# Two attention layers on one core: the attention output and its sums turned by 32x32 block transposes

## The reference

```python
# layer 0: 8 heads of 64, linear attention
q = softmax(q over d);  k = softmax(k over n)
att = einsum('bnhd,bnhl->bhdl', k, v);  y = einsum('bnhd,bhdl->bnhl', q, att)
x = x + silu(ln(y) * (1 + scale) + shift) @ W_out + b_out

# layer 1: 16 heads of 32, full attention over the 512 tokens of a batch
att = softmax(einsum('bnhl,bmhl->bnmh', q, k) + (1 - mask) * -1e6, axis=m)
y = einsum('bnmh,bmhl->bnhl', att, v)
out = x + silu(ln(y) * (1 + scale) + shift) @ out_w + out_b
```

## Time and profile before

| | us |
|---|---|
| median of 3 executions | 1419.43 |
| lowest and highest | 1418.87, 1429.26 |
| the profiled execution's own time | 1421.4 |
| its span, from first to last instruction | 1419.6 |

### The profile page before, as it was taken

One profiled execution on the slowest core, in us unless ns is written; L12 is line 12 of the kernel. 1 busy time (PEld: TensorE's weight loads), 2 busy tenths in 40 slices (PEclk: granted clock), 3 DMA queues, 4 the chain that ended last, 5 costly groups with the idle time before them and its releaser, 6 DMA issues.

```text
span 1419.6 us, 20550 instructions
## 1 busy us (share of the span) xinstructions
PE 1345.7 (95%) x7040; PEld 971.0 (68%) x7040; DVE 1005.0 (71%) x1966; ACT 821.8 (58%) x1429; POOL 770.8 (54%) x692
## 2 busy tenths in 40 slices
PE   6899999999999899999999999999999999999887
PEld 4678888888888786566666665666666666666445
DVE  5788978778788876677657657657757756756645
ACT  4255455454554644756756756756756766666663
POOL 0323243332433515467657757757847847846863
PEclk9899999999999999999999999999999999999999
DMA  9021111311213275745545535534634634633602
GB/s 336 1 67 53 46 60 38 97 60 38 68 37 111 91 216 172 221 135 161 143 132 160 156 119 163 165 119 145 182 120 139 182 104 142 200 105 112 180 14 82
DMA packets 82888, 172.93 MB, mean 122 GB/s; under 512 B 7240, under 2 KB 7240, under 8 KB 82784
## 3 DMA queue, kind: packets, MB, share of 16 engines
q1 hardware_dynamic: 82784, 171.62, 39.3%
HBM read 104.45 MB, written 67.14 MB: 121 GB/s over the span
## 4 chain that ended last, share of the span: by engine, by line
PE 65%; DVE 14%; DMA 7%; ACT 6%; issue 3%; POOL 3%; SPq 1%; DVEq 0%; POOLq 0%; ACTq 0%
PE ps L508 13%; PE ps L510 12%; PE ps L509 12%; PE ps L665 6%; PE ps L720 6%; PE ps L682 6%; DVE cT L1213 5%; PE ps L503 4%; DMA Ks<-stack_scratch 4%; PE ps L698 2%; DVE st L1052 2%; POOL yb L1392 2%; PE ps L596 1%; PE ps L617 1%; ACT xTh L786 1%
## 5 line engine op out<-in xcount | busy, mean ns | idle before, releaser
L1376 POOL TENSOR_TENSOR Pb<-Pb 128x512 f32<-128x512 f32 x376 | 470.2, 1289 | 218.4 <-PE ps L720 218.2
L1213 DVE TENSOR_REDUCE cT<-ps 128x1 f32<-128x512 f32 x512 | 326.2, 685 | 131.1 <-PE ps L665 126.3
L930 ACT ACTIVATE Pb<-ps 128x512 f32<-128x512 f32 x512 | 285.9, 602 | 190.3 <-PE ps L682 184.2
L665 PE MATMUL ps<-Ks,Qs 98*128 98x512 f32 x512 | 194.9, 419 | 10.9 <-DMA Ks<-stack_scratch 8.3
L682 PE MATMUL ps<-Qs,Ks 106*128 106x512 f32 x512 | 199.2, 415 | 2.3 <-ACT Qs L913 1.4
L665 PEld LDWEIGHTS ps<-Ks,Qs 98*128 98x128 f32 x512 | 95.4, 191 | 70.9 <-DVE cT L1213 21.4
L682 PEld LDWEIGHTS ps<-Qs,Ks 106*128 106x128 f32 x512 | 95.2, 190 | 50.7 <-issue 25.4
L1299 POOL TENSOR_TENSOR rs<-ve,mhalf 128x4 f32<-128x4 f32 x32 | 33.0, 1032 | 167.8 <-DVE ve L1038 115.3
L1327 POOL TENSOR_TENSOR vt<-vt,qmx 128x512 f32<-128x512 f32 x32 | 33.7, 1055 | 166.1 <-DVE qmx L1130 166.1
L508 PE MATMUL ps<-xTh,Wh_k 128*128 128x512 f32 x256 | 106.5, 416 | 3.6 <-DVE xTl L1065 2.3
L508 PE MATMUL ps<-Wh_o,sTh 128*128 128x512 f32 x256 | 106.3, 415 | 0.2 <-DVE sTl L1191 0.2
(11 more groups left out here) (176 smaller groups left out, 2956.1 us busy)
## 6 DMA issues: line engine op xcount, KB each, us to landing
Qs<-stack_scratch SPq DMA_DIRECT2D x32, 768.0 KB
Ks<-stack_scratch SPq DMA_DIRECT2D x32, 768.0 KB
stack_scratch<-sg_q SPq DMA_DIRECT2D x32, 512.0 KB, 2.7
stack_scratch<-sg_k SPq DMA_DIRECT2D x32, 512.0 KB, 2.8
wr<-in_x SPq DMA_DIRECT2D x32, 256.0 KB, 4.8
x_scratch<-wr SPq DMA_DIRECT2D x32, 256.0 KB, 2.0
stack_scratch<-sg_q SPq DMA_DIRECT2D x32, 256.0 KB, 2.9
stack_scratch<-sg_k SPq DMA_DIRECT2D x32, 256.0 KB, 3.5
```

The costliest lines, as they stand in the source:

```text
L665: e.matmul(bank[:], Qs[par][0:RX, j, t * 128:(t + 1) * 128], Ks[par][0:RX, j, :], start=True, stop=True).then_inc(s["S"], 1)
L930: e.activation(p_buf(n, m)[:, j, :], ps[bank_of["a", n, m, j]][:], ACT.Exp).then_inc(s["P"], 1)
L1213: e.tensor_reduce(nx[:, n % 2, j, t, 0:1], ps[bank_of["S", n, j, t]][:], AX.X, ALU.max, negate=True).then_inc(s["S_max"], 1)
L1376: e.tensor_tensor(acc[:, j, :], acc[:, j, :], p_buf(n, m)[:, j, :], ALU.add).then_inc(s["Ps_pool"], 1)
```

## The change

**Column tiles.** In `pv` each head's v is now loaded into all four column tiles, and column tile u takes the 128 tokens 128u to 128u+127 of that head: 16 matmuls with 128 moving columns for each m in place of 4 with 512. `den` does the same, with a `sel` that puts head h into row h of each quadrant. The bank `PV` then holds, in the 32 partitions of quadrant u, the 32 channels of head j at columns 128j and on, for the tokens of run u.

**Block transposes.** One DVE instruction turns the 32x32 blocks of `PV` straight into `yb` (`tl`, now DVE alone), and one turns the first 128 columns of `DEN` into `dt` in SBUF (`tlx`), from which the reciprocals are taken. The ACT copies L938, L946, L951 and the TensorE transposes behind them go.

**Order of the tokens.** After the block transposes, partition p = 32u + r of tile t holds token 128u + 32t + r. So that `x`, `k` and `v` stand in that order too, layer 1 loads its input from a second scratch `x1p`, which layer 0 stores beside `x1d`; the masks of layer 1 are turned on the host. The residual and the output keep the tokens' own order.

**Plan.** All of `PLAN`'s rows for layer 1 are new, and some for layer 0.

```diff
-    "tl": (0.2, 0.1, 0.9), "tlx": (1.0, 0.0, 0.4, 0.4, 0.4, 0.4),
+    "tl": (0.3,), "tlx": (0.1, 0.3, 0.4, 0.4, 0.4, 0.4),
...
-    "tl": (None, (0, 0.931), (0, 0.654), (0, 0.723)),
+    "tl": (None, (0.073, 1.091), (0.239, 0.802), (0.102, 0.771)),
...
+        x1p = nc.dram_tensor("x1_order_scratch", [B, 4, NT, 32, D], F32, kind="Internal").ap()
...
-        yt = vt[1]
+        dt = vt[1][:, 0:128]
...
                 for j in range(4):
-                    r = e.matmul(DEN[32 * j:32 * j + 32, :], sel[:, 4 - g:36 - g], p_buf(n, 0)[:, j, :],
-                                 start=(g == 0), stop=(g == NG - 1))
+                    h = 4 * g + j
+                    for u in range(4):
+                        r = e.matmul(DEN[32 * u:32 * u + 32, 0:128], sel[:, H1 - 1 - h:H1 + 31 - h],
+                                     p_buf(n, 0)[:, j, 128 * u:128 * u + 128], start=(h == 0), stop=(h == H1 - 1))
...
-                        r = e.matmul(PV[32 * j:32 * j + 32, :], xbuf(8 + b)[:, m, h * 32:(h + 1) * 32], pb[:, j, :],
-                                     start=(m == 0), stop=(m == NT - 1))
+                        for u in range(4):
+                            r = e.matmul(PV[32 * u:32 * u + 32, 128 * j:128 * j + 128], xbuf(8 + b)[:, m, h * 32:(h + 1) * 32],
+                                         pb[:, j, 128 * u:128 * u + 128], start=(m == 0 and j == 0),
+                                         stop=(m == NT - 1 and j == 3))
...
-            def tl(i, n):
-                b, g = divmod(n, NG)
-                if i == 1:
-                    e.wait_ge(s["yT"], n + 1)
-                    turn(PV, [yt[:, t * 128:(t + 1) * 128] for t in range(NT)]).then_inc(s["y1_tr"], 1)
...
-            def ae(i, n):
...
-                e.wait_ge(s["PV"], 4 * n + 4)
-                e.copy(yt[:], PV[:]).then_inc(s["yT"], 1)
...
+            def tl(i, n):
+
+                b, g = divmod(n, NG)
+                e.wait_ge(s["s_lo"], 4 * (7 + b) + g + 1)
+                e.wait_ge(s["PV"], 4 * n + 4)
+                e.transpose(yb[:, :, g * 128:(g + 1) * 128].rearrange("p t (j d) -> p j t d", j=4),
+                            PV[:].rearrange("p (j t r) -> p j t r", j=4, t=NT)).then_inc(s["y1"], 1)
+
             def tlx(i, b):
+                if i == 0:
+                    if b:
+                        e.wait_ge(s["rd"], b)
+                    e.wait_ge(s["den"], 4 * b + 4)
+                    e.transpose(dt, DEN[:, 0:128]).then_inc(s["dT"], 1)
...
-                    e.reciprocal(rd.rearrange("p t g j -> p t j g"),
-                                 DEN[:].rearrange("p (t j l) -> p t j l", t=NT, j=4)[:, :, :, 0:4]).then_inc(s["rd"], 1)
+                    e.reciprocal(rd, dt.rearrange("p (t h) -> p t h", t=NT)[:, :, 0:H1]).then_inc(s["rd"], 1)
...
-                src = (A["x"] if x < 8 else x1d)[x % 8]
+                src = A["x"][x] if x < 8 else x1p[x - 8].rearrange("u t r d -> (u t r) d")
...
+            def stored(x):
+
+                return 32 * min(x, B) + 16 * max(x - B, 0)
...
                     e.dma_start(dst[x % 8, t * 128:(t + 1) * 128, :], wr[t][:]).then_inc(s[f"st{t}"], 16)
+                    if x < 8:
+                        e.dma_start(x1p[x, :, t, :, :], wr[t][:]).then_inc(s[f"st{t}"], 16)
```

More of the change, by code:

```diff
@@ L368, in cond_two_layers @@
             "S", "S_max", "nx_set", "nx_hi", "nx_neg", "nx_lo", "nx_tr", "nxq", "ST", "P", "PV", "Ps_pool", "Ps_dve",
-            "yT", "y1_tr", "y1", "den", "dT", "d1_tr", "rd", "y1_sc")}
+            "y1", "den", "dT", "rd", "y1_sc")}
         def xbuf(x):
@@ L719, in pv @@
                         h = 4 * g + j
-                        r = e.matmul(PV[32 * j:32 * j + 32, :], xbuf(8 + b)[:, m, h * 32:(h + 1) * 32], pb[:, j, :],
-                                     start=(m == 0), stop=(m == NT - 1))
+                        for u in range(4):
+                            r = e.matmul(PV[32 * u:32 * u + 32, 128 * j:128 * j + 128], xbuf(8 + b)[:, m, h * 32:(h + 1) * 32],
+                                         pb[:, j, 128 * u:128 * u + 128], start=(m == 0 and j == 0),
+                                         stop=(m == NT - 1 and j == 3))
                     r.then_inc(s["PV"], 1)
-            def tl(i, n):
-                b, g = divmod(n, NG)
-                if i == 1:
-                    e.wait_ge(s["yT"], n + 1)
-                    turn(PV, [yt[:, t * 128:(t + 1) * 128] for t in range(NT)]).then_inc(s["y1_tr"], 1)
-            def tlx(i, b):
-                if i == 1:
-                    e.wait_ge(s["dT"], b + 1)
-                    turn(DEN, [yt[:, t * 128:(t + 1) * 128] for t in range(NT)]).then_inc(s["d1_tr"], 1)
             parts = {"m": m, "mb": mb, "tx": tx, "k": k, "v": v, "te": te, "q": q, "st": state, "y": y, "ty": ty, "o": o,
-                     "qk": qk, "S": S, "nxt": nxt, "a": a, "pv": pv, "den": den, "tl": tl, "tlx": tlx}
+                     "qk": qk, "S": S, "nxt": nxt, "a": a, "pv": pv, "den": den}
             for p, i in order:
@@ L930, in a @@
                 e.activation(p_buf(n, m)[:, j, :], ps[bank_of["a", n, m, j]][:], ACT.Exp).then_inc(s["P"], 1)
-            def ae(i, n):
-                if n:
-                    e.wait_ge(s["y1_tr"], n)
-                if n and n % NG == 0:
-                    e.wait_ge(s["d1_tr"], n // NG)
-                e.wait_ge(s["PV"], 4 * n + 4)
-                e.copy(yt[:], PV[:]).then_inc(s["yT"], 1)
-            def tl(i, n):
-                if i == 2:
-                    b, g = divmod(n, NG)
-                    if g == 0:
-                        e.wait_ge(s["s_lo"], 4 * (8 + b))
-                    e.wait_ge(s["y1_tr"], n + 1)
-                    e.copy(yb[:, :, g * 128:(g + 1) * 128], t4(PV)).then_inc(s["y1"], 1)
-            def tlx(i, b):
-                if i == 0:
-                    e.wait_ge(s["den"], 4 * b + 4)
-                    e.copy(yt[:], DEN[:]).then_inc(s["dT"], 1)
             parts = {"w": w, "nx": nx_, "ny": ny, "tx": tx, "k": k, "te": te, "v": v, "q": q, "sta": sta, "y": y, "ty": ty,
-                     "early": early, "stacks": stacks, "qk": qk, "nxt": nxt, "a": a, "ae": ae, "tl": tl, "tlx": tlx}
+                     "early": early, "stacks": stacks, "qk": qk, "nxt": nxt, "a": a}
             for p, i in order:
@@ L1565, in end @@
                 for t in range(4):
-                    e.wait_ge(s[f"st{t}"], 16 * 16)
+                    e.wait_ge(s[f"st{t}"], stored(16))
             prologue()
@@ L1585, in col, with turned @@
         return v.reshape(-1, 128).T
+    def turned(m):
+        return np.ascontiguousarray(m.reshape(B, NT, 4, 32).transpose(0, 2, 1, 3).reshape(B, T))
     def mcol(m):
@@ L1593 @@
         "m0": g["mask_BxSx1_fk1"].reshape(B, T),
-        "m1": g["mask_BxS_ff1"],
+        "m1": turned(g["mask_BxS_ff1"]),
         "mk": mcol(g["mask_BxSx1_fk1"]),
-        "mk1": mcol(g["mask_BxS_ff1"]),
+        "mk1": mcol(turned(g["mask_BxS_ff1"])),
         "cT": np.ascontiguousarray(g["cond_2048"].T.reshape(8, 128, B).transpose(1, 0, 2)),
```

48 lines of the change are left out of this document (24 added, 24 removed), and 14 rows, old and new, of the table PLAN.

## The result

The changed kernel takes 1460.62 us (median of 4 runs, 1453.65 to 1463.60). The kernel before, run beside it, takes 1422.68. The ratio is 1.0255, with an interval of 1.0197 to 1.0313: it is slower, by some 38 us, where the prediction's sum had 18 us of gain, and it lies outside the range given.

The account below looks back on a forecast made before the run. TensorE was taken as the limit, busy 95% of the span. Terms -20.0 - 4.1 + 4 + 2 + 1 - 1.1 = -18.2 from 1421.4 gave 1403.2, or 1401 us against the runs' median; range 1384 to 1424 us.

Parts of the forecast that it names:

- The second stores: Layer 0's 32 extra DMAs of 256 KB: +1 us, 3 without cover at the change of layers.
- What goes: TensorE loses 40 sets of transposes of PV and DEN, 20.0 us, and 4.1 us idle ahead of them.
- the gain is taken back by the queues: Rival: TensorE's waits move under the new plan and half the 24.1 us returns; no change, 1412 us; chance 0.20.
- What is added on TensorE: pv and den in four times as many matmuls, same columns: 3 ns for each of 1280 rounds, +4 us.
- the slow case: In pv and den, rounds too short to hide loads or issue; begun if 32 pv rows take over 1.02 us.
- short passes too short: Rival in pv and den: 0.11 us rounds cannot hide loads or issue; 1538 us with whole load exposed; chance 0.13.
- What is added on VectorE: Block transposes, 32 large at 0.69 us and 8 small at 0.30, delaying maxima TensorE waits for: +2 us.
- The new waits: On VectorE, the transpose waits for PV and GpSimd's s_lo, with the next group's maxima behind it; part of the VectorE step.
- the waits go as well: Rival: waits for turned sums and reciprocals shorten and half of TensorE's for maxima go; 1388 us; chance 0.12.
- The last stretch: Between the end of the sums and the reciprocal, a 0.30 us block transpose replaces 1.40 us: -1.1 us.
- The forecast of a batch, 106.6 us: Sign: a batch of layer 1 takes some 106.6 us in place of 109.
- layer 0 at 490 us: Sign of the prediction being right: layer 0 at 490 us.

Follow-up runs that it names:

- e2: The kernel before with only the second stores added, as the changed kernel issues them; nothing reads them: 1476.98 us, ratio 1.0392.
- e4: The changed kernel with its second stores in their own form, issued behind the load of the next input instead of ahead of it: 1432.74 us.
- e5: The kernel before with second stores of the same bytes in plain form (128 partitions outermost), which nothing reads: 1422.92 us, ratio 1.0020.
- e1: The changed kernel with each second store issued as four DMAs of 32 rows, same bytes to the same places: 1421.11 us, ratio 1.0003.
- e3: The changed kernel without second stores; layer 1 loads its input from x1d in permuted order, four DMAs a batch: 1404.13 us, ratio 0.9876.
- e7: e3 with the whole table PLAN of the kernel before: 1431.14 us, ratio 1.0066.
- e10: e7 with only the rows att and S of the changed kernel's table PLAN: 1434.01 us, ratio 1.0087.
- e9: The kernel before, turns and all, with the whole table PLAN of the changed kernel: 1465.25 us, ratio 1.0308.

## Why the prediction was wrong, point by point

**The step that failed is "The second stores".** It was to cost +1, up to 3, and it cost 57.1 in the profiled kernel, all ahead of layer 1; added alone to the kernel before, it cost 55 (e2). Two parts of its working fell. It was priced at "2.0 us to landing", but that row is of a store with 128 rows outermost; this one has 4 and was in no row, so by the working's own rule it needed bounds. A store of 256 KB on four engines at the 95 GB/s of the tail takes an estimated 2.8 us of those four, and the three ahead of the load 8.3 us, where a load alone needs 6.0 to land. That gives the size only: the first of the three had gone out 5.9 us ahead of the load, and how much was still queued then is not shown. And "Nothing in layer 0 reads them; the residual loads behind them are for the next batch" asked who reads the data, not what is queued behind it. The load of the next input is (e4), as the rows of SP's order had shown ahead of the prediction; its statistics stand in VectorE's order ahead of this batch's `ql`, and TensorE needs `ql`. "SP spends 0.37 us on an issue" was near for a wide second store (0.43 to 0.49 in e5) and harmless there, but not when each store is cut in four (e1); a narrow one took 0.51 us, and 1.37 to 2.43 when others stood close ahead of it (202.37 and 268.26 us, after). What stays open is why TensorE's clock fell as it did: 16.1 of the 57.1 us are slower matmuls, a cost for which the step had no term.

**What goes, -24.1.** Right in sum, not as a law. In the stretch of six batches above, TensorE's busy time fell by 14.4 us in e3 and its idle time by 3.5. But "a microsecond of TensorE's stream that goes is worth nearly a microsecond" holds only where the order around it is fitted anew: under the old table the freed time came back as waits and 10 us more (e7). The rival "the gain is taken back by the queues" named that mechanism, and the new table is what kept it from happening. That the sum came out is to that extent luck: no step of the working asked whether the new table was needed for it. The rival's price, half of the gain, was too small for e7.

**What is added on TensorE, +4.** Near: some 2.6, by steps of 0.02 and 0.03 us that the timeline's hundredths just resolve. TensorE's timeline after, around a run of sums and `pv`, which answers to the earlier trace rows:

```profile
1057.33 1.08 PE L702 MATMUL ps<-Pb,sel 128*32 128x128 f32 x32
1058.23 1.93 PE L725 MATMUL ps<-Pb,xin 128*32 128x128 f32 x64
1060.09 0.50 PE L684 MATMUL ps<-Qs,Ks 106*128 106x512 f32 x1
```

The 32 rows of sums take 0.90 us (0.88 before) and the 64 rows of `pv`, a pair of m, 1.86 (1.83), way out included: 32 x 0.02 + 64 x 0.03 = 2.6 us. 32 rows in half of 1.86, 0.93, lie near the 0.88 that was to show it right and under the 1.02 of the slow case. So the loads are hidden beside passes of 128 columns, and the rival "short passes too short" falls: a slower kernel came, but from another place. Groups by shape after, for the earlier trace rows:

```profile
L725 PE MATMUL ps<-Pb,vf 128*32 128x128 f32 x2048 | 64.5, 278 | 2.9 <-ACT Pb L925 2.9
...
L725 PEld LDWEIGHTS ps<-Pb,vf 128*32 128x32 f32 x2048 | 55.8, 112 | 10.6 <-ACT Pb L925 6.1 <-issue 3.4
```

The busy time of the group is 64.5 for 63.1, in four times as many rows. 64 rows in 1.86 us are one per 29 ns. The Trainium skill ("TensorE: Matmul & The Clock Gate", section "Step-by-step: what each phase is for", on decode and dispatch) has some 62 ns a MATMUL where hardware decode is off; the trace does not show that limit here.

**What is added on VectorE, +2.** The prices were near: 0.71 us for the large transpose (0.69 given), from the groups after, and 0.32 for the small one (0.30), in the timeline of the last stretch below.

```profile
L1231 DVE STREAM_TRANSPOSE yb<-ps 128x512 f32<-128x512 f32 x32 | 22.6, 707 | 12.1 <-PE ps L725 12.1
```

The Trainium skill ("VectorE: DVE Perf Modes", section on the three transpose paths) gives 311 ns for 128x128 in bf16; the 0.32 us of this float32 one is near it.

The new waits came where they were named: the large transposes waited 12.1 us for `PV` in all. What TensorE waits for maxima did not grow to 23 or 24 us in the row that stood for it, but fell from 21.4 to 12.4. Part of it moved: the same wait at the score products (L682, now L684) grew from 7.2 to 11.4, and the one of `nxt` for `nxs` from 10.3 to 13.1. What the transposes cost TensorE by themselves was not taken apart. Waits of layer 1 after, 604 to 1440 us:

```profile
POOL yb L1378 <- DVE cU L1246: 30.1, 8, 6.8
...
PEld ps L667 <- DVE cT L1187: 12.4, 42, 0.4
```

GpSimd's wait for the reciprocals fell from 45.0 to 30.1, in the direction of "the waits go as well"; that rival's whole price of 13 us more did not come.

**The last stretch, -1.1.** Right: from the start of the small transpose to that of the reciprocal are 0.42 us, where 1.40 stood, so -0.98.

```profile
1429.67 0.32 DVE L1239 STREAM_TRANSPOSE vt<-ps 128x128 f32<-128x128 f32 x1 [1.58 <-PE ps L702]
...
1430.09 0.55 DVE L1246 RECIPROCAL cU<-vt 128x64 f32<-128x64 f32 x1
```

The last batch ahead of it is 3.9 us longer (51.2 for 47.3 from its first sums to its last `pv`), which no step foresaw; e10 points to two rows of the table for some 3 of it.

**The sum without the failed term.** By the terms -20.0, -4.1, +4 and +2, -18.1 over eight batches, the seven later ones were to give 15.8 us; they gave 14.7. The forecast of a batch, 106.6 us, stands against 742.4 us from the first sums of one batch to those of the next, seven times: 106.1 (759.9 and 108.6 before). By the prediction's own sign for being wrong, a batch of 108 us or more, layer 1 was right; of its signs only "layer 0 at 490 us" looked at the stores.

## What to carry to other kernels

Price a new DMA by its form before its bytes: look at the outermost dimension of both sides, and when it is small, as 4 was here, ask what is issued behind it on the same queue, and which in-order engine stands at that transfer with other work behind it. That nobody reads a store says nothing on what it delays. And work taken off the limiting engine has a price only together with the order of work around it: an order fitted to a kernel can lose more than the work is worth when the work goes (e7) or when the order changes alone (e9), so change both, and measure the four cells. And look at the granted clock beside the waits: in three of these runs (after, e9, e10) matmuls at a lower clock took 11 to 18 us that no row of waits shows.

## What the runs showed of the hardware

- A store of 256 KB with 4 x 32 x 512 at its destination left DMA at a share of 0.25 and 95 GB/s, where the burst of before moved 264 GB/s. A 1 MB load issued behind such stores landed in 11.6 us in place of 6.0, and issued ahead of them in 6.3.
- TensorE's granted clock fell to 0.74 in the 6 us in which it stood (2.4 and 1.2 GHz mixed), and was 0.77 in the 8 us after. Up to layer 1 the same products took 16.1 us longer, beside 41.0 of idle time. In e9 they took 17.5 us longer over six batches at 0.97 for 1.00.
- Four column tiles took 64 rows of matmul of 128 columns in 1.86 us, with a load of 110 to 112 ns ahead of each, where 16 rows of 512 columns took 1.83: all but 0.03 us of the loads is hidden.
